# Layer norm statistics over two interleaved tiles per instruction, without aggregation

## The reference

```python
def _layernorm(x, axis=-1, eps=1e-05):
    m = jnp.mean(x, axis=axis, keepdims=True)
    v = jnp.var(x, axis=axis, keepdims=True)
    return (x - m) / jnp.sqrt(v + eps)
```

## Time and profile before

| | |
|---|---|
| median of 3 runs | 4019.06 us (4015.88 to 4021.55) |
| the profiled execution | 4020.56 us |
| its span | 4018.8 us |
| PE busy | 3075.4 us, 77% of the span |
| DVE busy | 3290.3 us, 82%, 9625 instructions |
| ACT busy | 2173.0 us, 54% |
| POOL busy | 2085.5 us, 52% |
| DMA | 679.72 MB, mean 169 GB/s |

### The profile page before, as it was taken

How to read it: one execution, slowest core, us unless ns; L and a number is a source line. 1 busy time by engine, 2 the same in 40 slices (tenths; PEclk the granted TensorE clock), 3 DMA queues, 4 the chain that set the end, 5 groups by cost and what they waited for, 6 DMA issues and landing times. The chain is left out here.

```text
span 4018.8 us, 66244 instructions
## 1 busy us (share of the span) xinstructions
PE 3075.4 (77%) x13334; PEld 1749.4 (44%) x13334; DVE 3290.3 (82%) x9625; ACT 2173.0 (54%) x5748; POOL 2085.5 (52%) x2017
## 2 busy tenths in 40 slices
PE   4866757777749997569995658999979999218886
PEld 1255644444424443124442545555546666104443
DVE  6979979999969997768786877888956666779997
ACT  0048868999952322442221776777746666115554
POOL 5945557766637551037660006666645555006676
PEclk9967778999969998889997888999989999659998
DMA  2069987877742221689993994555545565213332
GB/s 56 3 189 311 308 268 234 253 246 245 246 118 74 69 69 36 183 226 278 282 276 103 287 268 108 143 143 142 137 148 194 197 199 190 68 46 112 114 113 86
DMA packets 635184, 679.72 MB, mean 169 GB/s; under 512 B 168901, under 2 KB 496159, under 8 KB 628581
## 3 DMA queue, kind: packets, MB, share of 16 engines
q1 hardware_dynamic: 587012, 575.17, 45.7%
q0 software_dynamic: 48000, 102.76, 11.6%
HBM read 385.35 MB, written 296.91 MB: 170 GB/s over the span
## 5 line engine op out<-in xcount | busy, mean ns | idle before, releaser
L1411 PE MATMUL r_pM<-r_masked,wr 128*128 128x512 f32 x1600 | 712.8, 596 | 10.7 <-DVE r_masked L1356 10.7
L1356 DVE SCALAR_TENSOR_TENSOR r_masked<-r_typ,r_hT 128x512 f32<-128x512 f32 x800 | 495.4, 690 | 101.7 <-ACT r_hT L1389 78.7
L1411 PEld LDWEIGHTS r_pM<-r_masked,wr 128*128 128x128 f32 x1600 | 295.4, 191 | 357.4 <-issue 291.9
L691 POOL DMA_INDIRECT q_rows<-nr,row_x x200 | 259.2, 1296 | 194.8 <-PE q_pT L600 134.5
L2432 POOL DMA_INDIRECT out<-o_base,o_at_o x200 | 266.1, 1331 | 134.4 <-issue 66.3
L691 POOL DMA_INDIRECT r_xs<-h_tab,r_at_s x200 | 229.9, 1149 | 87.7 <-issue 47.0
L691 POOL DMA_INDIRECT r_xs<-tab,r_at_s x200 | 212.1, 1060 | 87.9 <-issue 46.5
L691 POOL DMA_INDIRECT e_zd<-xz,dst_c x200 | 191.7, 959 | 90.4 <-issue 52.6
L691 POOL DMA_INDIRECT i_hs<-hr,i_at_s x200 | 191.3, 957 | 87.8 <-issue 47.1
L2240 ACT ACTIVATE q_eo<-q_pO,b 128x512 f32<-128x512 f32 x196 | 134.7, 687 | 172.5 <-PE q_pO L2275 148.8
L691 POOL DMA_INDIRECT e_zs<-xz,src_c x200 | 190.4, 952 | 71.0 <-issue 59.1
(11 more groups left out here) (426 smaller groups left out, 9141.8 us busy)
## 6 DMA issues: line engine op xcount, KB each, us to landing
xz<-na_xz SPq DMA_DIRECT2D x49, 1040.0 KB, 5.8
r_typ<-vec_s SPq DMA_DIRECT2D x100, 256.0 KB, 4.5
g_al<-alpha_s SPq DMA_DIRECT2D x100, 256.0 KB, 4.3
na_xz<-in_x SPq DMA_DIRECT2D x49, 512.0 KB, 6.9
tab<-na_x SPq DMA_DIRECT2D x49, 512.0 KB, 2.8
e_xin<-tab SPq DMA_DIRECT2D x49, 512.0 KB
hr<-e_hh SPq DMA_DIRECT2D x49, 512.0 KB, 3.2
nr<-e_n SPq DMA_DIRECT2D x49, 512.0 KB
```

The lines of the kernel that those rows point to most:

```text
L691: pool.indirect_dma_start(dest[:, j, :], None, table, bass.IndirectOffsetOnAxis(ap=index[:, j:j + 1], axis=0), element_offset=first).then_ ...
L1356: v.scalar_tensor_tensor(masked[:, r, :], typ[d.slot(4)][:, :], float(r), hT[d.slot(2)][:, :], ALU.is_equal, ALU.mult).then_inc(ev.mk, 1)
L1411: pe.matmul(pM[s][:, :], g.wr[:, layer * R_ + r, :], masked[:, r, :], start=(r == 0), stop=(r == R_ - 1)).then_inc(ev.mm, 1)
```

## The change

Every layer norm's statistics are taken of two tiles by one bn_stats. Its input is read with the tile index innermost (x of tile j, feature 0; x of tile j+1, feature 0; x of tile j, feature 1, and so on), so that its even elements are one tile and its odd elements the other. The six numbers that it writes are then count, mean and sum of squared deviations of either tile, and go straight into mv, which has three columns for each tile instead of two. There is no bn_aggr, no buffer st and no wait between. Whoever read the variance reads the sum of squared deviations with a factor of 1/128, and the means are read from column 1.

```diff
-def stats(v, c, g, x4, st, mv, done):
+def stats(v, x, mv, done):
+    for j in range(0, x.shape[1], 2):
+        last = v.bn_stats(mv[:, j:j + 2, :].rearrange("p t c -> p (t c)"), x[:, j:j + 2, :].rearrange("p t f -> p f t"))
+    last.then_inc(done, 1)
 def rstd(a, g, c, mv, rs, done):
-    c.step(a.activation(rs[:, :], mv[:, :, 1], ACT.Ln, bias=g.eps_ln[:, :]))
+    c.step(a.activation(rs[:, :], mv[:, :, 2], ACT.Ln, bias=g.eps_ln[:, :], scale=1.0 / P))
 def normalise(v, x4, mv, rs, y4, done):
-        last = v.tensor_scalar(y4[:, j, :], x4[:, j, :], mv[:, j, 0:1], rs[:, j:j + 1], ALU.subtract, ALU.mult)
+        last = v.tensor_scalar(y4[:, j, :], x4[:, j, :], mv[:, j, 1:2], rs[:, j:j + 1], ALU.subtract, ALU.mult)
-def pair_stats(v, c, g, x8, st, mv, done):
-    for j in range(2 * J):
-        last = v.bn_stats(st[:, j, :], x8(j))
-    c.step(last)
-    v.sem_inc(g.state.waits, 1)
-    for j in range(2 * J):
-        last = v.bn_aggr(mv[:, j, :], st[:, j, :])
-    last.then_inc(done, 1)
...
# node_rows
-                    pair_stats(v, c, g, lambda j: rows[:, j, 0:P], st, mv[s], ev.st)
+                    stats(v, rows[:, :, 0:P], mv[s], ev.st)
-                    v.tensor_scalar(ve[s][:, :], mv[s][:, :, 1], EPS_LN, None, ALU.add).then_inc(ev.ve, 1)
+                    v.tensor_scalar(ve[s][:, :], mv[s][:, :, 2], 1.0 / P, EPS_LN, ALU.mult, ALU.add).then_inc(ev.ve, 1)
...
# layer0_edges
-                    pair_stats(v, c, g, lambda j: z_tile(n1, j), stz, mvz, nd.sz)
+                    for j in range(0, 2 * J, 2):
+                        last = v.bn_stats(mvz[:, j:j + 2, :].rearrange("p t c -> p (t c)"), z_tiles(n1, j).rearrange("p (t f) -> p f t", t=2))
+                    last.then_inc(nd.sz, 1)
-                    pair_stats(v, c, g, lambda j: hh[n2.slot(4)][:, j, :], sth, mvh, nd.sh)
+                    stats(v, hh[n2.slot(4)], mvh, nd.sh)
...
```

More of the change, by code:

```diff
@@ L799, in node_rows @@
         y, junk, et, aT = (sb(n, [P, 2 * J, P]) for n in ("y", "junk", "et", "aT"))
-        st = sb("st", [P, 2 * J, 6])
-        mv = some("mv", 2, [P, 2 * J, 2])
+        mv = some("mv", 2, [P, 2 * J, 3])
         ve, rs, bw, ss, tq, rq, q = (some(n, 2, [P, 2 * J]) for n in ("ve", "rs", "bw", "ss", "tq", "rq", "q"))
@@ L885, in turn @@
                         v.wait_ge(ev.t1, p.back(1, m))
-                        v.tensor_tensor(y[:, of(m), :], rows[:, of(m), 0:P], mv[s][:, of(m), 0:1].broadcast_to([P, J, P]), ALU.subtract).then_inc(ev.ya, 1)
+                        v.tensor_tensor(y[:, of(m), :], rows[:, of(m), 0:P], mv[s][:, of(m), 1:2].broadcast_to([P, J, P]), ALU.subtract).then_inc(ev.ya, 1)
                 p = pair(3)
@@ L991, in layer0_edges @@
         hh, n_ = some("hh", 4, [P, 2 * J, P]), some("n", 4, [P, 2 * J, P])
-        stz, sth = (sb(n, [P, 2 * J, 6]) for n in ("stz", "sth"))
-        mvz, mvh = (sb(n, [P, 2 * J, 2]) for n in ("mvz", "mvh"))
+        mvz, mvh = (sb(n, [P, 2 * J, 3]) for n in ("mvz", "mvh"))
         rz, nm, rh = (sb(n, [P, 2 * J]) for n in ("rz", "nm", "rh"))
@@ L1277, in relations @@
         masked = sb("masked", [P, R_, HW])
-        st, mv, rs = sb("st", [P, J, 6]), some("mv", 2, [P, J, 2]), some("rs", 2, [P, J])
+        mv, rs = some("mv", 2, [P, J, 3]), some("rs", 2, [P, J])
         kq, recent = sb("kq", [P, HW]), some("recent", GROUP, [P, HW])
@@ L1337, in _ @@
             v.memset(pK[:, :], 0.0).then_inc(s_0, 1)
-            c = Chain(v, s_v, line.unroll if layer == 0 else 0)
             def turn(pair, at):
@@ L1363, in turn @@
                     v.tensor_tensor(z[s][:, :, :], z[s][:, :, :], hh[p.slot(2)][:, :, :], ALU.add).then_inc(zz, 1)
-            line.sweep(v, turn, c)
+            line.sweep(v, turn)
         @block.scalar
@@ L1699, in aggregate_rows @@
         rows, hh = some("rows", 4, [P, J, P]), some("hh", 2, [P, J, P])
-        st, mv = sb("st", [P, J, 6]), some("mv", 2, [P, J, 2])
+        mv = some("mv", 2, [P, J, 3])
         rs, nm = some("rs", 2, [P, J]), some("nm", 2, [P, J])
@@ L1735, in _ @@
             v.wait_ge(s_0, 1)
-            c = Chain(v, s_v, line.unroll)
             def turn(at):
@@ L1752, in turn @@
                     v.wait_ge(ev.nm, d.back(2))
-                    stats(v, c, g, rows[d.slot(4)], st, mv[s], ev.st)
+                    stats(v, rows[d.slot(4)], mv[s], ev.st)
                 d = at(5)
@@ L1758, in turn @@
                     v.wait_ge(ev.hh, d.back(2))
-                    v.scalar_tensor_tensor(nm[s][:, :], mv[s][:, :, 0], -1.0, rs[s][:, :], ALU.mult, ALU.mult).then_inc(ev.nm, 1)
-            line.sweep(v, turn, c)
+                    v.scalar_tensor_tensor(nm[s][:, :], mv[s][:, :, 1], -1.0, rs[s][:, :], ALU.mult, ALU.mult).then_inc(ev.nm, 1)
+            line.sweep(v, turn)
         @block.scalar
@@ L1917, in _ @@
             v.wait_ge(s_0, 1)
-            c = Chain(v, s_v, 4 * line.unroll)
+            c = Chain(v, s_v, 2 * line.unroll)
             def turn(at):
```

27 lines of the change are left out of this document (12 added, 15 removed).

## The result

On the same chip the changed kernel took 3929.53 us (median of 4 runs, 3926.56 to 3931.19) against 4017.47 us of the kernel before (4014.98 to 4021.55): a ratio of 0.9779, 95% interval 0.9762 to 0.9796. Two more chips look like that one by the kernel before and by edited kernels; the changed kernel itself was not run on them.

The account below looks back on a forecast made before the run. DVE was taken to bound layer0_edges and node_rows, with other engines or transfers covering the rest. Gains of 34 us in layer0_edges, 9 in node_rows and 2 at stage ends made 45, so 4019.06 became 3974 us, range 3950 to 4010.

Parts of the forecast that it names:

- the price of the jump: Every new bn_stats: the interleaved read of a tile pair costs 526 ns, at 1.79 ns per element; 52% chance.
- ACT's floor in layer0_edges: layer0_edges: once DVE is relieved, ACT can go no faster than 10.2 us a turn.
- the cap on node_rows: node_rows: transfers leave room for only some 325 GB/s, a turn of 6.57 us, so 17 us gain at most.
- the two stages: Only node_rows and layer0_edges get shorter in their steady parts, by 9 and 34 us.
- the covers: relations, aggregate_rows and interaction gain nothing, hidden behind PE, the transfers and the chain to the scan.
- the nearest row: Reduction over relations in edge_softmax, jumping among eight streams: 3006 ns for 1600 elements, taken as the price of the new read.
- jumps between only two streams are free: Rival for every new bn_stats: a pair costs 337 ns, gaining 57 us in all, 3962 us; 28% chance.
- the 510 ns of the page: Estimate for the new bn_stats from the Trainium skill's 1.73 ns per element; would move the sum by under 2 us.
- two waits of 0.84 us: layer0_edges: ACT's waits for DVE, 0.84 us a turn each, subtracted from its turn to get 10.2 us.
- the ends: First and last turns of the five stages, where a result's delay counts: 2 us gain.
- The forecast growth of that wait: interaction: the wait of i_agg for i_pL gets longer by some 0.6 us a turn.
- the prediction's caps: Limits on the gain: ACT at 10.2 to 10.3 us a turn in layer0_edges, transfers at some 325 GB/s in node_rows.

Follow-up runs that it names:

- the probe: Changed kernel plus an added stage near its start timing read orders in groups of eight equal DVE instructions; 4395.57 us beside 4176.98 for the kernel before.
- only_rest: Kernel before with the new statistics in relations, aggregate_rows and interaction alone; 4017.89 us, ratio 0.9991.
- before_again: The kernel before, unchanged, run once more on a chip of the slower kind; 4194.22 us.
- pool_less2: Changed kernel with seven gathers a turn in layer0_edges instead of eight, on a slower chip; 4168.77 us, 0.9918 of the kernel before.
- merged_with_aggr: Kernel before with half its bn_stats, each over two interleaved tiles, every bn_aggr and wait kept, on a slower chip; 4162.53 us, ratio 0.992.
- after_again: The changed kernel, unchanged, run once more on a slower chip; 4308.8 us, 1.0257 of the kernel before.
- no_zs: Changed kernel without the four source-row gathers a turn in layer0_edges, on a chip like the first; 4078.76 us, 1.0136 of the kernel before.

## Why the prediction was wrong

Three terms of the sum were mis-sized, and all on the same side: the price of the jump, ACT's floor in layer0_edges, and the cap on node_rows. The direction, the two stages and the covers were right.

**The price of the jump** is the step that failed first. 526 ns were taken from the eight-stream reduction as the nearest row; measured are 354 ns in the kernel, and 416 against 411 ns of duration beside a contiguous read in the probe. The rival "jumps between only two streams are free" was true, in PSUM too, for the reason that it gave: the row's streams were eight, and the fourth already costs. It had 28% and should have had more, since its one difference to the row was one in kind. A smaller slip stands beside it: at the 510 ns of the page that it cites, ten instructions take 0.16 us less in a turn, which by the prediction's own floors is some 4 us in layer0_edges, and not under 2.

**layer0_edges**: bound and order of the next ones were right (DVE, then ACT, then POOL), but ACT's floor was mis-sized: 10.2 us were forecast, 9.95 to 9.98 measured. The prediction took two waits of 0.84 us off the turn of 11.04. But ACT's busy time was 45.2 of 50 us, 9.98 in a turn, so it was idle for 1.06, and its busy time alone would have given the floor. The waits of the earlier trace rows are gone, and the busy time is even a little shorter, 49.05 / 5.01 = 9.8 us a turn; that instructions which don't wait overlap more is a likely reason, not a shown one. The stage gave 51.6 us for 34 (forecast) or 38 (rival).

**node_rows** failed twice. 0.25 us a turn were expected from DVE by the price above, 1.01 by the free one, and measured are 1.01 (2.47 to 1.46) between the two rows, of which the turn kept 0.70. And the cap of 325 GB/s, which held the rival's gain at 17 us, was set by feeling for a share above 1: the stage runs at 347 to 355 GB/s in all its stretches. A share of 1.04 was no sign of the end; what came with the higher rate is the issue time of a transfer, 0.36 us before and 2.3 to 2.6 in the turns after. The Trainium skill's DMA: Bandwidth & Descriptors, section Specifications, gives about 358 GB/s as a core's limit to HBM, which these rows approach; by it the rival's turn would have been an estimated 5.95 us, where 6.01 was measured; that this limit holds the stage is not shown. The stage's turn of before was also read from one example of 6.91 us, while (580.1 - 258.2) / 48 is 6.71 from the first to the last of na_x. Gain: 35.6 us for 9 (forecast) or 17 (rival).

**relations, aggregate_rows, interaction** held: 0.7, 2.4 (with edge_softmax) and 1.3 us, and only_rest gave 4 in all with the ends. The reasons held too: PE full, the transfer of the output, i_pL. The forecast growth of that wait was 0.6 us a turn, measured 0.93.

The rival's price with the prediction's caps gives its 57 us. The price of 526 ns without the caps would give 49 x 0.75 + 49 x 0.25 + 2, or 51. Only the rival's price joined to the measured turns gives 49 x 1.09 + 49 x 0.7 + 2, or 90 us. So no single term explains the miss: the price is worth 12 us of it with the caps as they were, and the caps the other 33.

## What to carry over

An instruction that takes two tiles through its even and odd halves pays next to nothing for the interleaving (354 ns for 349), and saves half the fixed parts and the whole aggregation; with four or more streams in SBUF that would not hold. Price an access by a row with the same number of streams, not merely one that also jumps. When a bound is taken away, work out the next floors from a stretch's busy time and one from its waits, and take a transfer cap only from a rate that has been seen to stall something. And a gain on one chip is not yet a gain: run both kernels on another before shipping. Where a wait seems to have no cause, read when the semaphore was raised before taking a modelled end of PE for its real one.

## What was not expected of the hardware

- The chips fell into two kinds. On two, and in the first comparison, whose chip is not on record, the kernel before takes 4017 to 4022 us, on three others 4177 to 4202, and nearly all of the surplus is in layer0_edges (155 of 174 us in before_again). There the ratio of the change turns from 0.978 to 1.026. Shown is that the changed stage is the longer one there although ACT's and POOL's instructions are as fast as on the first chip (e_et 0.72 us, gathers 1.25 us apart), and that in each gap the semaphores of PE's e_pY and e_pX come up to 17 us late. Why they do is open, and so is why SyncE's issues take 3 to 6 us. ACT's program, the bytes of e_xin and a lighter ACT were tried and change nothing. pool_less2, with seven gathers, and merged_with_aggr, with more work on DVE, have shorter turns than after_again (14.19 and 12.96 us against 16.54), so the pace or density of the gathers may matter; that is argued. Untested are pauses forced into the run of gathers, no_zs on such a chip, PE's turns in a loop, and what other load the chip had.
- bn_stats reads a step of 4 words at 592 ns and one of 24 words at 778 ns for 256 elements, against 411 contiguous, while hopping 4096 words to and fro between two streams costs 8 ns.
